# Two layers with adapters on one core: other orders in the engines' programs of the setup and of the first batch

## The reference

```python
low = jnp.einsum('bsi,bir->bsr', x, lora_A[labeler_index])
x = x + einsum('bsi,oi->bso', x, W0) + einsum('bsr,or->bso', low, lora_B_w) * (16 / 32)
lora_h = jnp.einsum('bti,bir->btr', x, lora_As[adapter_mapping])
x = x + einsum('bti,oi->bto', x, W1) + b + einsum('btr,bro->bto', lora_h, lora_Bs[adapter_mapping]) * (32 / 16)
```

## Time and profile before

| | |
|---|---|
| median of 3 runs | 330.77 us (330.41 to 330.86) |
| profiled execution, its own time | 329.88 us |
| its span, first to last instruction | 328.0 us |
| mean granted clock of TensorE | 0.969 of full speed |
| TensorE busy | 305.5 us |
| VectorE busy | 235.0 us |
| ScalarE busy | 139.7 us |
| GpSimd busy | 70.3 us |

### The profile page before, as it was taken

How to read it: one execution, slowest core, us unless ns; L and a number is a source line. 1 busy time by engine, 2 the same in 40 slices (tenths; PEclk the granted TensorE clock), 3 DMA queues, 4 the chain that set the end, 5 groups by cost and what they waited for, 6 DMA issues and landing times.

```text
span 328.0 us, 4334 instructions
## 1 busy us (share of the span) xinstructions
PE 305.5 (93%) x1397; PEld 248.6 (76%) x1397; DVE 235.0 (72%) x310; ACT 139.7 (43%) x223; POOL 70.3 (21%) x84
## 2 busy tenths in 40 slices
PE   6984999899994999967999999999999999999995
PEld 5873888688883888846887878878878878878874
DVE  3539882888999859996487598588587687677331
ACT  4654345939506346613424424424424524435110
POOL 4613000000002620143007007016025034043000
PEclk9995999999998799995999999999999999999999
DMA  6999400610004400027208327226346255203002
GB/s 202 267 355 242 56 0 3 108 21 2 0 0 82 73 0 0 1 48 154 80 16 155 112 37 163 88 46 146 88 65 159 56 82 141 56 0 128 0 22 107
DMA packets 99362, 27.55 MB, mean 84 GB/s; under 512 B 84885, under 2 KB 93077, under 8 KB 99350
## 3 DMA queue, kind: packets, MB, share of 16 engines
q1 hardware_dynamic: 99350, 27.41, 35.9%
HBM read 19.01 MB, written 8.39 MB: 84 GB/s over the span
## 4 chain that ended last, share of the span: by engine, by line
PE 80%; DVE 9%; ACT 4%; issue 3%; POOL 1%; DMA 1%; SPq 0%; DVEq 0%; POOLq 0%
PE bank L983 78%; PE bank L1005 2%; ACT vt_hi L418 1%; DVE xt L815 1%; DMA a<-in_L_cond_W 1%; DVE s_lo L618 1%; DVE vt L618 1%; DVE t L618 1%; DVE v L618 1%; DVE a_lo L618 1%; DVE vt_lo L618 1%; ACT p_hi L418 1%; PE bank L1170 1%; ACT ym L418 1%; ACT a_hi L418 0%
## 5 line engine op out<-in xcount | busy, mean ns | idle before, releaser
L983 PE MATMUL bank<-vt_hi,s_hi 128*128 128x512 f32 x96 | 37.4, 390 | 0.0
L983 PE MATMUL bank<-vt_lo,s_hi 128*128 128x512 f32 x96 | 37.4, 390 | 0.0
L983 PE MATMUL bank<-vt_hi,s_lo 128*128 128x512 f32 x96 | 37.3, 389 | 0.0
L815 DVE STREAM_TRANSPOSE xt<-raw 128x512 int32<-128x512 int32 x32 | 32.2, 1080 | 0.0
L418 ACT ACTIVATE lhs_hi<-xt 128x512 fp32r<-128x512 f32 x32 | 19.8, 628 | 27.3 <-PE bank L983 17.8
L618 DVE TENSOR_TENSOR lhs_lo<-xt,lhs_hi 128x512 fp32r<-128x512 f32 x32 | 27.5, 867 | 4.2 <-ACT lhs_hi L418 3.8
L618 DVE TENSOR_TENSOR s_lo<-s_sum,s_hi 128x512 fp32r<-128x512 f32 x32 | 27.5, 883 | 2.9 <-ACT s_hi L418 2.9
L418 ACT ACTIVATE s_hi<-s_sum 128x512 fp32r<-128x512 f32 x32 | 19.7, 627 | 18.7 <-PE bank L983 9.9
L983 PE MATMUL bank<-v_hi,lhs_hi 128*128 128x512 f32 x64 | 25.0, 390 | 1.2 <-issue 1.2
L983 PE MATMUL bank<-v_lo,lhs_hi 128*128 128x512 f32 x64 | 25.8, 404 | 0.0
L983 PE MATMUL bank<-t_hi,s_hi 128*128 128x512 f32 x48 | 20.5, 428 | 5.3 <-DVE s_lo L618 5.3
(11 more groups left out here) (163 smaller groups left out, 755.5 us busy)
## 6 DMA issues: line engine op xcount, KB each, us to landing
raw<-in_x SPq DMA_DIRECT2D x32, 256.0 KB, 4.8
out<-y SPq DMA_DIRECT2D x32, 256.0 KB, 2.1
n<-in_L_cond_W SPq DMA_DIRECT2D x16, 256.0 KB, 5.3
a<-in_L_cond_W SPq DMA_DIRECT2D x16, 256.0 KB, 5.3
a_raw<-in_L_cond_lora_A SPq DMA_DIRECT2D x8, 128.0 KB, 2.3
a_raw<-in_L_cond_lora_As SPq DMA_DIRECT2D x8, 64.0 KB, 2.4
b_raw<-in_L_cond_lora_Bs SPq DMA_DIRECT2D x8, 64.0 KB, 2.1
b_raw<-in_L_cond_lora_B_w SPq DMA_DIRECT2D x1, 128.0 KB, 6.6
```

The source lines that it names most:

```text
L815: nc.vector.transpose(xt[:, n, :, :].rearrange("p e (s sb) -> p sb e s", sb=GR).bitcast(I32), rows[:, n // 2, n % 2].bitcast(I32)).then_in ...
L983: return nc.tensor.matmul(ps, lhsT, rhs, start=start, stop=stop, skip_group_check=more)
```

## The change

No operation is added or taken away, and the shapes are the same. What changes is the place of operations in the programs of four engines, and with them some waits:

- TensorE: b11's fourth block is turned ahead of `vm1(1)`; b22's and b12's turns stand between the parts of `vm1`, whose last block is cut in two halves (rows 0, 1 and rows 2, 3); the q products against b11 stand ahead of b12's last turn.
- VectorE: `b0_lo` ahead of `t1_t3`; `t1_t3(2)` ahead of `t3_low(0)`; a1's parts ahead of b21's; `vt23(1)` ahead of t4's low parts, the x quarters 1 and 3; the first batch's `s_low` and `b1_low` ahead of v22.
- ScalarE: a1's high part ahead of b21; a12's ahead of `ym`; the copy into `ac` behind the first batch's quarters; `s_high` and `b1_high` of the first batch ahead of v22.
- GpSimd: `ac` is zeroed ahead of `b1_raw`; the first batch's sums stand ahead of c's columns.

SP's queue keeps its order; its wait ahead of the bias is for the sixth zeroing in place of the fifth, which is the same one (`b1_raw`).

```diff
@@ sync
-            sp.wait_ge(zeroed, 5)
+            sp.wait_ge(zeroed, 6)
@@ gpsimd
+            pool.wait_ge(q_done, 2)
+            pool.wait_ge(b0a1_done, 1)
+            pool.wait_ge(w0_eyed, 2 * HK)
+            nc.gpsimd.memset(ac[:, :, :].bitcast(F32), 0.0).then_inc(zeroed, 1)
             pool.wait_ge(ct_done, 2)
-            pool.wait_ge(w0_eyed, 2 * HK)
+            pool.wait_ge(zeroed, 5)
             nc.gpsimd.memset(b1_raw[96:128, :], 0.0).then_inc(zeroed, 1)
+            pool.wait_ge(zeroed, 6)
...
-            pool.wait_ge(q_done, 2)
-            pool.wait_ge(b0a1_done, 1)
-            pool.wait_ge(zeroed, 5)
-            nc.gpsimd.memset(ac[:, :, :].bitcast(F32), 0.0).then_inc(zeroed, 1)
+            pool.wait_ge(v_done, M3 + HK)
+            sums(0)
             pool.wait_ge(c_lo_made, 2)
-            pool.wait_ge(zeroed, 6)
             adapter_columns(0)
             pool.wait_ge(b0a1_all_made, 1)
             b0a1_columns(0)
-
-            pool.wait_ge(v_done, M3 + HK)
-            sums(0)
@@ scalar
+            act.wait_ge(a1_in, 16 * B)
+            copy(a1_hi[:, :, :], a1_raw[:, :, :, :].rearrange("p t b r -> p t (b r)"), a1_hi_made, LORA1_SCALE)
...
-            for m in range(HK):
-                act.wait_ge(v_done, M6 + m + 1)
-                bank_copy(ym, m, LOW[m], vy_made)
+            act.wait_ge(v_done, M6 + HK)
             for j in range(HK):
                 act.wait_ge(a12_in[j], 16)
                 high(a12_hi, a12, j, w0_hi_made)
+            for m in range(HK):
+                bank_copy(ym, m, LOW[m], vy_made)
...
-            act.wait_ge(zeroed, 6)
-            a0_high(0)
...
+            act.wait_ge(zeroed, 5)
+            a0_high(0)
+            for j in range(4):
+                s_high(0, j)
+            act.wait_ge(bias_in, 16)
+            act.wait_ge(p_ql_made, 2)
+            b1_high(0)
+            act.wait_ge(v_done, M5 + HK)
+            for m in range(HK):
                 bank_copy(v22_hi, m, LOW[m], v22_hi_made)
@@ vector
+            dve.wait_ge(b0s_made, 1)
+            dve.wait_ge(b0_hi_made, 1)
+            tt(b0_st[:, :, 64:64 + R0], b0_raw[:, :, :], b0_st[:, :, 0:R0].bitcast(F32), ALU.subtract, b0_lo_made)
...
             s3_sum(0)
+            t1_t3(2)
             t3_low(0)
-            t1_t3(2)
             s3_low(0)
...
-            for j in range(HK):
-                dve.wait_ge(w1_hi_made, HK + j + 1)
-                tt(b21_lo[:, j, :], TURN_BANK[j % 3][:, :], b21_hi[:, j, :].bitcast(F32), ALU.subtract, w1_lo_made)
...
             tt(a1d[:, :, :], raw_a1[:, HK:KT, :], raw_a1[:, 0:HK, :], ALU.subtract, a1d_made)
+            for j in range(HK):
+                dve.wait_ge(w1_hi_made, HK + j + 1)
+                tt(b21_lo[:, j, :], TURN_BANK[j % 3][:, :], b21_hi[:, j, :].bitcast(F32), ALU.subtract, w1_lo_made)
...
             vt23(0)
+            vt23(1)
             for h in range(2):
                 dve.wait_ge(t_hi_made, T4_AT + h + 1)
                 low(t4_lo, t4, t4_hi, PAIR[h], t_lo_made)
-            vt23(1)
+            vt23(2)
             dve.wait_ge(q_done, 2)
-            turn_x(0, range(2))
-            vt23(2)
-            turn_x(0, range(2, 4))
+            turn_x(0, range(1))
             vt23(3)
+            turn_x(0, range(1, 4))
...
+            for j in range(4):
+                s_low(0, j)
+            b1_low(0)
@@ tensor
-            vm1(0)
+            vm1(0, range(HK))
             turn_b11(2)
-            vm1(1)
             turn_b11(3)
-            vm1(2)
+            vm1(1, range(HK))
             turn_b22(0)
+            vm1(2, range(HK))
             turn_b22(1)
-            vm1(3)
             turn_b22(2)
+            vm1(3, range(0, 2))
             turn_b22(3)
-            for j in range(HK):
-                turn_b12(j)
+            turn_b12(0)
+            vm1(3, range(2, HK))
+            turn_b12(1)
+            turn_b12(2)
+
+            pe.wait_ge(b0_lo_made, 1)
+            for j in range(HK):
+                q_step(Q_BANK[0], j, B11, j, j == 0, False)
+            turn_b12(3)
```

More of the change, by code:

```diff
@@ L469, in _ @@
                 bank_copy(b21, j, TURN_BANK[j % 3], w1_made)
-            act.wait_ge(a1_in, 16 * B)
-            copy(a1_hi[:, :, :], a1_raw[:, :, :, :].rearrange("p t b r -> p t (b r)"), a1_hi_made, LORA1_SCALE)
-            for m in range(HK):
-                act.wait_ge(v_done, M6 + m + 1)
-                bank_copy(ym, m, LOW[m], vy_made)
+            act.wait_ge(v_done, M6 + HK)
             for j in range(HK):
@@ L554, in _ @@
                 a_high(0, g)
+            act.wait_ge(zeroed, 5)
[6 more added lines that the diff above has]
+            act.wait_ge(v_done, M5 + HK)
             for m in range(HK):
-                act.wait_ge(v_done, M5 + HK)
                 bank_copy(v22_hi, m, LOW[m], v22_hi_made)
@@ L560, in _ @@
                 copy(vt1_hi[:, m, :], vt1[:, m, :], vt1_hi_made)
-            for j in range(4):
-                s_high(0, j)
             act.wait_ge(v_done, M4 + HK)
@@ L574, in batch @@
                     a_high(b, 3)
[L575 to L578, removed]
+                    b1_high(b)
                 act.wait_ge(m1_done, b + 1)
@@ L744, in _ @@
             s3_low(1)
-            dve.wait_ge(b0s_made, 1)
-            dve.wait_ge(b0_hi_made, 1)
-            tt(b0_st[:, :, 64:64 + R0], b0_raw[:, :, :], b0_st[:, :, 0:R0].bitcast(F32), ALU.subtract, b0_lo_made)
             for h in range(2):
@@ L904, in _ @@
                 low(vt1_lo, vt1, vt1_hi, m, vt1_lo_made)
-            v21_vt4(0)
-            s_low(0, 0)
-            s_low(0, 1)
-            v21_vt4(1)
-            s_low(0, 2)
-            s_low(0, 3)
-            v21_vt4(2)
-            v21_vt4(3)
+            for m in range(HK):
+                v21_vt4(m)
             for m in range(HK):
@@ L924, in batch @@
                     a_low(b, 3)
-                b1_low(b)
+                    b1_low(b)
                 dve.wait_ge(m6_done, b + 1)
@@ L1039, in _, with vm1 @@
             T1, T2, T3, T4 = (t1_hi, t1_lo), (t2_hi, t2_lo), (t3_hi, t3_lo), (t4_hi, t4_lo)
-            def vm1(j):
+            def vm1(j, rows):
                 pe.wait_ge(w1_lo_made, j + 1)
                 pe.wait_ge(w0_lo_made, j + 1)
-                for m in range(HK):
+                for m in rows:
                     last = step(LOW[m], A11, B11, j, m, j == 0, j == HK - 1)
@@ L1107, in _ @@
             turn_b21(HK - 1)
-            pe.wait_ge(b0_lo_made, 1)
-            for j in range(HK):
-                q_step(Q_BANK[0], j, B11, j, j == 0, False)
             pe.wait_ge(w1_lo_made, 2 * HK)
```

## The result

The changed kernel takes 322.21 us (median of 4 runs, 320.79 to 322.37) beside 330.59 us of the kernel before on the same chip (4 runs, 329.92 to 330.86): a ratio of 0.974 (95% interval 0.971 to 0.977), 8.4 us less. The prediction said 325.3, in a range of 321.0 to 327.5. The profiled execution took 322.18 us, with a span of 320.4 us and a mean granted clock of 0.984 (0.969 before). In the table of the experiments the ratio leaves out one execution each of e5_ac (326.03 us) and e10_ac_12 (324.63 us), which took over 1.5% longer than the fastest of their kernel; the median has them in.

A forecast was written before the change was run, and what follows sets the result against it. VectorE was taken to bound the stretch until u_st releases TensorE's low-rank product: 2.0 + 5.7 - 2.3 = 5.4 us off 330.77 gives 325.4, written 325.3; forecast itself 324.0 to 326.7, range 321.0 to 327.5.

The forecast's parts named there:

- rival (a): Ahead of u_total the clock falls earlier and is back at 2.4 GHz for the low-rank product: 322.4 us, chance 0.2.
- Part 1: Front: TensorE's turns reordered, q products and b0_lo moved into idle time; 1.0 us gained on VectorE.
- part 2: Middle: a1 ahead of b21, a12 ahead of ym; VectorE 2.0 us ahead at the last v sum, front included.
- Part 3: Late first batch: ac cleared early removes 5.7 us of VectorE waits; moved GpSimd sums cost 2.3 us.
- four waits of 5.7 us: VectorE's waits ahead of vt_lo, two c_lo and the first v_lo: 0.52, 1.16, 0.16 and 3.84 us, all to go.
- rival (b): At the moved sums, GpSimd takes nothing more from VectorE, so 2.3 us less: 323.0 us, chance 0.1.
- the 325.7: Time if each further sum beside vt_lo costs VectorE its full length, 2.6 us in place of 2.3.
- Cost nothing as long as VectorE has no gap: Other reorderings in VectorE's full stretch (vt23(1), x quarters, s_low, b1_low) were to cost nothing.
- another idle stretch of 1 to 2 us follows: Argument against rival (a): TensorE idles again after its longer wait ahead of u_total.
- Rival (c): The new wait for b21's fourth b_lo lets the clock fall, cancelling part 2's gain: 327.2 us, chance 0.12.
- (d): The removed waits are taken up by others, time within 0.2% of before: 330.8 us, chance 0.03.
- (e): Front: n11's last load lands late for b11's fourth block; 3 us late gives 328.3 us, chance 0.05.

The follow-up runs named there:

- e5_ac: The kernel before with only GpSimd's zeroing of ac moved ahead, behind the second q product: 321.32 us, ratio 0.971.
- e10_ac_12: The kernel before with Part 1, part 2 and the early zeroing of ac; sums, s_low, b1_low, s_high, b1_high in their old places: 321.13 us, ratio 0.974.
- e8: The changed kernel with eight turns of eye instead of four between b11's first two blocks on TensorE: 321.52 us, ratio 0.972.
- e7: The changed kernel with 28 unused turns of eye on TensorE ahead of its wait for u_sum (u_total): 323.55 us, ratio 0.979.
- e1: The kernel before with only TensorE's new front order and VectorE's b0_lo and t1_t3(2) moved: 326.75 us, ratio 0.988.
- e11: The kernel before with ac zeroed early and GpSimd's first-batch sums moved ahead of c's columns, nothing else: 325.60 us, ratio 0.985.
- e6: The changed kernel with GpSimd's first-batch sums held until b1's low part, behind c's columns, and s_high and s_low behind vt1: 319.63 us, ratio 0.966.
- e4: The kernel before with 28 unused turns of eye on TensorE ahead of the first batch's wait for u_st: 328.94 us, ratio 0.995.
- e9: e6 with 28 unused turns of eye on TensorE ahead of the first batch's wait for u_st: 316.50 us, ratio 0.959.
- e2: The kernel before with only a1 ahead of b21 and a12 ahead of ym, on ScalarE and VectorE: 326.49 us, ratio 0.988.
- e3: The kernel before with all late edits of the four engines, front and middle as before: 324.97 us, ratio 0.986.

## Why the prediction was right, and where its sizes were off

The measured 322.21 us lie outside the forecast itself, 324.0 to 326.7. They lie in the range because the range reached down to rival (a), and two other errors, 1.05 us too much at the last `v` sum and 0.7 us too little behind it, partly cancelled: that part is luck.

**What bounds the kernel: right.** In all kernels the low-rank product is released by `u_st`, and VectorE's gains arrive there.

**Part 1 and part 2, 2.0 us at the last `v` sum: right in the order's effect, 0.95 us in this execution.** The first quarter of A11·B11 ran slowly in the profiled execution (last section), some 1.4 us at TensorE's front, and so the first t was at 21.86, not 20.9, and `s_lo` ended at 29.57, not 28.6. Where the front was fast, the same orders have the last `v` sum at 79.97 (e8), 79.59 (e7) and 79.54 (e10): 2.1 to 2.6 us ahead of 82.09. `q_part` at 61.15 instead of 60.05 is the same 1.1 us. "Have no wait for `ct`, a new one of about 1.5 us for `b_lo`" and 3.2 us for `s_lo`: measured none, 1.4 and 3.3.

**Part 3, 5.7 less 2.3 us: 4.1 us measured instead of 3.4** (5.05 at `u_sum` less 0.95). All four waits of 5.7 us went. The price of a sum beside back-to-back `vt_lo` was predicted at 1.15 us (with the 0.61 us that the text names, give 1.16 and 1.32), and four of them cost 9.29 - 4.90 = 4.4, 1.10 each; four `vt_lo` took 1.77 to 1.78 us, as predicted (1.8). The two slow `lhs_lo` of before are fast now (2.67 for four, where e1 still has 5.02 and the kernel before 5.03, a gain of 2.4). So the net price against before is 2.0 where the text had 2.3: rival (b) fell. By the rule of the Trainium skill that the prediction quoted (SBUF — State Buffer, "Who interferes with whom") each sum would cost its full 1.28 us, four of them 5.1, by an estimate from that rule (the 325.7 there counts from 325.4; from the 325.3 that was written it is 325.6). The 4.4 and 4.0 us measured are nearer to the row's price. 5.7 - 2.0 leaves 0.4 of the 4.1 us; 0.2 of it is in the last four `vt_lo` (2.48 us instead of 2.68), the rest in steps of 0.1 us and less.

**"Cost nothing as long as VectorE has no gap": wrong as a judgement of the edit.** The prediction compared the sums' new place with the old one as it was in the kernel before, where two of them hurt. It didn't ask where they would lie if only `ac` were cleared early. e5 shows that they would hurt nobody, e11 that moving them costs VectorE 4.0 us, of which 2.1 arrive, and e6 that the changed kernel without this loss has its low-rank product 4.2 us sooner behind the first t. One edit of the change carries the gain, and another gives back as much as parts 1 and 2 bring.

**The clock: the step that failed.** The forecast kept the half clock behind the low-rank product and gave 0.2 to rival (a), 322.4. Rival (a) is what happened: the fall went to the idle time ahead of `u_total` (3.35 us, predicted 2 to 4), and the rest is 2.7 us shorter (2.9 predicted). The argument against it, that "another idle stretch of 1 to 2 us follows", didn't hold: 0.6 us followed, since the slow products filled it. e4 and e9 show the term by itself (178.5 and 178.4 to 175.8). Rival (c) fell: behind the `b_lo` wait of 1.4 us the products (from 56.53) follow each other at 0.23 us, the full rate. Rivals (d) and (e) didn't occur.

By these steps the span goes from 328.0 by 0.95 + 4.1 = 5.05 at `u_sum`, of which 4.9 reach the low-rank product, and by 2.7 for the clock, to 320.4.

What stays open: why the fall goes with a wait of 3.3 us in some executions and not in others (e2, e5 and e7 had the full clock behind one), and so how much of the differences between the medians of e1, e2, e5 and e10 is the order's. The fall can also come late: in e10 TensorE waited only 1.2 us ahead of `u_total`, worked again from 133.96, and the clock fell at about 135.9; the seven products from 135.95 took the half speed, and the low-rank product at 140.99 had the full clock. So there the half speed lay under the free products without a long wait ahead of them.

## What to carry to other kernels

When several edits come together, price each against the program with the others in it, not against the program before: a contention that the profile shows may vanish by itself when its neighbour stops being late, and the edit meant beside it may bring it back. Put GpSimd's operations on SBUF beside VectorE operations that read a bank. And read where the clock's fall lies: half speed under products that nobody waits for was free here, and an otherwise idle wait ahead of the bound stretch can be filled with useless turns, which took 2.7 us off the rest in both kernels that had them.

## What the runs showed of the hardware that I had not expected

- The contention of VectorE and GpSimd has two outcomes for the same operations. In the changed kernel, e7 and e8 they alternate (eight `vt_lo` in 9.29 to 9.30 us, four of them slowed in the changed kernel, one for each sum; sums of 1.49 to 1.74, only e7's first one 2.70), in e3 VectorE keeps its pace (4.91) and one sum of 1.28 us takes 5.68. The same holds for the copy of `c_hi` into `ac`: 2.83 us beside `lhs_lo` in e5, 0.42 in the changed kernel. In e3 the sum began 0.37 us after the first `vt_lo`, in the changed kernel 0.34 us; what decides isn't settled.
- The front is slow in some executions (the changed kernel, e2, e4, e11) and not in others: the first products then follow each other at 0.43 us instead of 0.23, as here, while the granted clock of the same stretch reads 1.00. TensorE's timeline, and its half microseconds, of the changed kernel:

```profile
7.31 0.78 PE L980 MATMUL bank<-b_hi,a_hi 128*128 128x512 f32 x1
...
8.31 0.63 PE L980 MATMUL bank<-b_hi,a_lo 128*128 128x512 f32 x1
8.73 0.63 PE L980 MATMUL bank<-b_hi,a_hi 128*128 128x512 f32 x1
...
10.75 0.39 PE L980 MATMUL bank<-b_hi,a_lo 128*128 128x512 f32 x1
```

```profile
7.50:8.00 0.50, 0.50 (x3) 1.00 1.02 341
10.00:10.50 0.50, 0.50 (x3) 1.00 1.23 304
```

The record of the clock doesn't show this slow stretch; the spacing of the products does.
